# Order of the pieces in a round of the 16-head attention: other work between the scores and the values

## The reference, cut to what matters

```python
qkv = (x @ W_qkv + b_qkv).reshape(B, S, 3, H, hd)          # H = 16, hd = 8
attn = softmax(einsum('bqhd,bkhd->bhqk', q, k) / sqrt(hd))
attn_out = einsum('bhqk,bkhd->bqhd', attn, v)
moe_out = sum over e of (x @ W_experts[e] + b_experts[e]) * combine[e]
return attn_out + moe_out
```

## Time and profile before

| | us |
|---|---|
| median of 3 runs | 1065.94 (1064.5 to 1068.49) |
| the profiled execution, its own time | 1064.29 |
| its span, first to last instruction | 1062.5 |
| TensorE busy | 980.8 (92%) |
| ScalarE busy | 757.9 (71%) |
| VectorE busy | 568.7 (54%) |
| the rounds of the four sequences, in the trace | 151.41, 151.38, 151.35, 147.85 |

### The profile page before, as it was taken

The page is one execution under the profiler, slowest core; times in us unless marked ns, Lnnn a source line. Parts: engine busy times, 40 slices in busy tenths (PEclk is TensorE's granted clock), DMA queues, the critical chain, the costliest instruction groups (busy, mean ns, idle before and its releaser), DMA issues.

```text
span 1062.5 us, 16258 instructions
## 1 busy us (share of the span) xinstructions
PE 980.8 (92%) x6122; PEld 548.3 (52%) x6122; DVE 568.7 (54%) x1377; ACT 757.9 (71%) x922; POOL 203.9 (19%) x144
## 2 busy tenths in 40 slices
PE   2699899999999989999989989999998998999995
PEld 1588743344378853334347875334436886333431
DVE  6845744554465663472654574456447357346352
ACT  5253589988853479997955357998894436999885
POOL 3200021322120020240230002043022001114123
PEclk9799999999999989999999998999999999999998
DMA  6000033000000013200000002300000000320000
GB/s 236 1 2 1 1 49 62 1 2 1 1 22 2 1 19 50 43 2 2 1 20 2 1 1 39 51 22 1 1 1 21 2 1 10 50 33 1 1 1 23
DMA packets 14428, 20.66 MB, mean 19 GB/s; under 512 B 2848, under 2 KB 11136, under 8 KB 14080
## 3 DMA queue, kind: packets, MB, share of 16 engines
q1 hardware_dynamic: 14336, 19.41, 8.5%
HBM read 7.85 MB, written 2.10 MB: 9 GB/s over the span
## 4 chain that ended last, share of the span: by engine, by line
PE 72%; DVE 9%; ACT 6%; issue 6%; SPq 4%; POOL 2%; DMA 1%; DVEq 0%; POOLq 0%; ACTq 0%
PE ps L1090 69%; SPq L351 4%; ACT big L1046 3%; PE ps L1489 1%; DVE st L275 1%; DVE mx L483 1%; POOL st L866 1%; DVE xn L451 1%; DVE wk L731 1%; DVE wk L541 1%; ACT xn L1018 1%; DVE flags L419 1%; DVE wk L476 1%; PE ps L1110 1%; DVE qk_max L556 0%
## 5 line engine op out<-in xcount | busy, mean ns | idle before, releaser
L1046 ACT ACTIVATE big<-ps 128x1024 f32<-128x1024 f32 x512 | 493.8, 1034 | 50.5 <-PE ps L1090 48.6
L1090 PE MATMUL ps<-big,vaug 128*32 128x512 f32 x2048 | 272.6, 604 | 3.7 <-DVE wk L731 2.5
L1090 PE MATMUL ps<-hid 32*128 32x512 f32 x1024 | 130.5, 493 | 3.5 <-ACT big L1046 1.9
L1090 PE MATMUL ps<-hid,fw_sb 128*128 128x512 f32 x416 | 100.6, 396 | 0.0
L866 POOL TENSOR_TENSOR st<-st 128x4 f32<-128x4 f32 x16 | 16.2, 1011 | 433.9 <-DVE st L530 325.8
L965 ACT ACTIVATE wk<-ps,cols_sb 128x512 f32<-128x512 f32 x64 | 40.5, 687 | 78.3 <-PE ps L1090 74.2
L1090 PEld LDWEIGHTS ps<-hid 32*128 32x128 f32 x1024 | 49.1, 181 | 77.1 <-issue 42.0
L1090 PEld LDWEIGHTS ps<-hid,fw_sb 128*128 128x128 f32 x416 | 77.8, 188 | 17.6
L879 POOL TENSOR_TENSOR qz<-qz,wk 128x512 f32<-128x512 f32 x32 | 41.2, 1287 | 232.6 <-DVE wk L701 232.6
L1090 PEld LDWEIGHTS ps<-big,vaug 128*32 128x32 f32 x2048 | 41.0, 108 | 69.7 <-issue 41.6
L719 DVE SCALAR_TENSOR_TENSOR big<-ps,sm,big 128x128 f32<-128x128 f32 x128 | 44.2, 346 | 46.6 <-PE ps L1090 35.9
(11 more groups left out here) (210 smaller groups left out, 1630.5 us busy)
## 6 DMA issues: line engine op xcount, KB each, us to landing
hid<-spl SPq DMA_DIRECT2D x288, 32.0 KB
xnext<-in_x SPq DMA_DIRECT2D x4, 512.0 KB, 3.9
out<-qz SPq DMA_DIRECT2D x8, 256.0 KB, 2.3
big<-in_fw SPq DMA_DIRECT2D x1, 1877.0 KB, 9.2
wk<-in_lw SPq DMA_DIRECT2D x1, 1476.0 KB, 14.3
big<-in_fw SPq DMA_DIRECT2D x1, 939.0 KB, 11.0
cst_sb<-in_cst SPq DMA_DIRECT2D x1, 440.0 KB, 4.5
xn<-in_aw SPq DMA_DIRECT2D x1, 320.0 KB, 5.2
```

Source lines behind the costliest of these rows:

```text
L1046: up(ms_exp, a.activation(prob[:, at:at + 2 * CH].rearrange("p (h n) -> p h n", n=CH), ps[:, bank:bank + 2, :], ACT.Exp, scale=HDM ** -0.5))
L1090: return t_.matmul(out_, lhsT, rhs, start=start, stop=stop, **kw)
```

## The change

The call of `m_values` moves from before the side piece to behind it, on TensorE alone. The other engines' lists, all semaphores and the table `SIDE` stay as they are.

```diff
                 for k_ in range(CYCLES):
                     if k_ < QUADS:
                         m_scores(k_)
-                    if LAG <= k_ < QUADS + LAG:
-                        m_values(k_ - LAG)
                     what, i = side_piece(b, k_)
                     if what == "qk":
...
                         up(r_mm, split3(side, gh_hi[:, 0:D], gh_lo[:, 0:D], *xT(i)))
+                    if LAG <= k_ < QUADS + LAG:
+                        m_values(k_ - LAG)
```

## The result

The changed kernel takes 1104.71 us (median of 4 runs, 1103.18 to 1106.97), the kernel before 1065.22 beside it: a ratio of 1.0355 with an interval of 1.0323 to 1.0387. The forecast was 1106. The profiled execution took 1103.65 us, its span is 1101.9, where the sum of the forecast said 1104.8.

What follows compares the result with a forecast made beforehand. It took TensorE's matmuls to bound the rounds (busy 146.35 of 151.38 us). Terms 28.2 + 8.0 + 4.3 = 40.5 us on the profiled 1064.29 gave 1104.8, and 1106 with the median 1.65 above; range 1086 to 1122.

Steps and rivals of the forecast that it cites:

- The beat: Steady rounds: same matmuls and neighbouring pairs, piece to piece stays 2.33 us; cost taken as 0.
- Term 1: Rounds 9 to 57: VectorE's copy, ahead of its piece part, delays the next piece; 7.04 us per sequence, 28.2 in all.
- Term 2: Rounds 2, 4, 7, 14: pieces wait for ScalarE's work, no longer covered by values; 2.00 us per sequence, 8.0 in all.
- Term 3: End of the rounds: `nat7` and the next sequence come 1.44 us later; three sequences, 4.3 us.
- Absorbed waits: Rival: half of the copy's waits in the rounds is caught up later, giving 1092 us; chance 0.10.
- The clock: Rival: new waits drop TensorE's clock once per sequence in the rounds, +14 us, giving 1120; chance 0.08.
- a sign that it is wrong: Within the rounds: a fall of the granted clock would show the prediction wrong; no size given.
- Faster: Rival: earlier pieces win at most all 5.0 us of idle TensorE per sequence, 20 us, giving 1046; chance 0.03.
- no difference: Rival: the change only renames waits, each hidden under slack, giving 1066 us; chance 0.03.

Runs made afterwards that it cites:

- the parts: Three runs, the kernel before with values behind the piece only in rounds 0 to 15, 16 to 61 or 62 to 65: 1074.49, 1091.67, 1070.86 us.
- the mirror image: The kernel before with VectorE's copy moved behind its part of the side piece, TensorE's order unchanged: 1126.34 us, ratio 1.0568.
- the mixed version: The kernel before with values behind the piece and VectorE's copy behind its part of the piece, in rounds 16 to 61 only: 1068.9 us, ratio 1.0008.

## Why the prediction was right

Growth in the rounds of the first sequence, in us, read from the starts of its scores before and after:

| step of the forecast | foretold | measured |
|---|---|---|
| copy at round 9 (`head_logits`) | 0.62 | 0.55 |
| copies at 17, 25, 33 | 0.79, 0.54, 0.76 | 0.74, 0.71, 0.77 |
| copies at 41, 49, 57 (experts) | 1.59, 1.15, 1.59 | 1.55, 1.03, 1.55 |
| pieces that need ScalarE: rounds 2, 4, 7, 14 | 0.58, 0.43, 0.40, 0.59 | 0.57, 0.35, 0.39, 0.63 |
| end of the rounds | 1.44 | 1.18 |

- *The beat costs nothing.* Right: rounds 44 to 47 take 10.09 us where they took 10.08, so the direction in which the shapes are passed costs nothing over a round; the single steps were not taken apart.
- *Term 1, the copy.* 6.9 us a sequence, 27.6 in all, for 28.2. Putting the copy behind the piece gives it back, 28.9 with the clock's share. Round 25's copy was sized by following ScalarE's backlog through, and came out 0.17 low.
- *Term 2, ScalarE's cover.* 1.94 a sequence, 7.8 in all, for 8.0. Shown twice: rounds 0 to 15 alone cost what terms 1 and 2 say of them (9.8), and ScalarE's part ahead of its second exponential takes back rounds 4 and 7 whole and 0.50 of round 14's 0.63. Round 2's 0.57 stays there, so for that one the cause is read from the timeline alone: the piece waits for L541, and that for L994.
- *Term 3, the end.* 3.5 us for 4.3. The mechanism is right (rounds 62 to 65 alone: +3.7), two terms were too large: I took 1.00 for the first of the two values groups at the end, as if a piece of another shape followed. It is followed by values, and the step is 564.92 - 564.04 = 0.88. And the copy starts 1.11, not 1.20, behind the second.
- *Absorbed waits.* The rival of 1092 falls: the parts add up, 40.8 against 40.2.
- *The clock.* It fell once in the rounds, at 547, for 1.55 us (the second sequence grew by 11.54, the third by 9.98), not once a sequence for 3.5. The forecast had 0 for it, and had named a fall within the rounds as a sign that it is wrong: by that sign this term was missed, for 1.55 us of 40. The rival was priced too high for this kernel, but isn't idle: with the copy made twice, and in the mirror image, it cost some 14 and 15 us.
- *Faster, and no difference.* Neither: the spacing from piece to piece, 2.33 in both orders, left nothing to win.

27.6 + 7.8 + 3.5 + 1.55 are 40.4, the rounds show 40.2. That this is so near the forecast's 40.5 is partly luck: the three terms came out 1.6 us too large together, and the fall of the clock, which had no term, put as much back. From the 40.2, less 0.8 outside the rounds, come the 39.4 by which the profiled execution grew. Outside, the part between the first two sequences' rounds took 102.79 for 103.72 us: the stretch of the lower clock ahead of the second sequence's rounds did not come in this execution. Why it stayed away isn't known.

## What to carry to other kernels

Where engines work through written lists, moving an operation on one of them moves a wait onto whatever stands behind its counterpart on the others. The reader of the result, and the work whose result comes late, must move with it. The costing that held here went from event to event: when the operand arrives, what is queued behind the waiting instruction, and which slack swallows it. An order is only free once all lists agree on it; then, here, it is worth nothing that the timed runs can tell, either way. And a new order changes what runs side by side: the scan beside GpSimd's instruction was in no list of waits, and took back the gain of the mixed version.

## What the runs showed of the hardware

- The granted clock. Of the changed kernel's twelve waits of 1.4 to 1.5 us behind the experts, in rounds that are otherwise full, eleven left it at 2.4 GHz and one was followed by 3.4 us at 1.2 GHz; with the new order in rounds 16 to 61 alone it was again one of twelve. With the copy made twice it fell in nine places: behind all four waits of 2.08 us in round 42, three of the four of 1.62 in round 26 and two of the four of 1.41 in round 18, but behind none in rounds 34, 50 and 58, of 1.51, 2.01 and 2.08. In the mirror image it fell with six of the eight waits of 2.43 to 2.52 us, and with none of those of 1.65. So longer waits bring more falls, and a slightly longer wait cost more than its length (14 of the 33 us of the second copy), but the length alone doesn't decide, and what does isn't shown. The Trainium skill, "TensorE: Matmul & The Clock Gate", Part 1, warns that idle gaps put the engine back to half rate; the runs agree, and show that gaps this short can do it, not always.
- VectorE beside GpSimd. L701, a scan of 128x512, takes 1.22 to 1.29 us in all 295 places of the twelve traces where nothing of GpSimd's runs beside it. Where GpSimd's tensor_tensor of 128x512 overlaps it for 0.27 us it takes 1.35, for 0.72 us 1.80, for 0.98 us 2.06 and for 1.27 us 2.39. The spans of GpSimd in a trace are rough, and no run takes the pair apart; but the scan grows with the overlap by nearly as much as the overlap.
- A queued copy of 0.69 us holds up VectorE's next instruction for 0.60 (503.84 to 504.44), and the first of the doubled copies holds the second for 0.61 (520.21 to 520.82): the recorded length is more than the list pays for it.
